# Eight joint VectorE sums per tile moved ahead of chosen multiplies in a pairwise-interaction recommender kernel

## The chip, the cores and the metric

The kernel runs on one core of one Trainium2 chip. The metric is the device time of one execution in microseconds (us). A core has five engines that run side by side and meet through semaphores: TensorE (PE, with its weight loads shown as PEld), VectorE (DVE), ScalarE (ACT), GpSimd (POOL) and SyncE (SP), which here only issues transfers.

## What is computed

32 table lookups per row give embeddings of 64 numbers, every pair of fields is combined through its own 64 x 64 matrix into one number, and the 496 numbers with 16 dense ones pass a small network:

```
e = stack([tbl_f[ids[:, f]] for f in range(32)], axis=1)      # 1024 x 32 x 64, float32
p = e[:, ROW_IDX]; q = e[:, COL_IDX]                           # the 496 pairs of fields
z = einsum('bne,hne,bnh->bn', p, kernel, q)                    # kernel 64 x 496 x 64
h = concatenate([z, dense_ctx], axis=1)                        # 1024 x 512
h = maximum(h @ W_top1 + b_top1, 0)                            # 512 x 512
h = maximum(h @ W_top2 + b_top2, 0)                            # 512 x 256
y = h @ W_top3                                                 # 256 x 1
```

## The kernel before

**Tiles and blocks.** The batch of 1024 rows is worked off in 8 tiles of 128 rows, numbered 0 to 7. Within a tile the 496 pairs are cut into 32 blocks, numbered 0 to 31. For each block TensorE writes a product `u` of embeddings and pair matrices (`block_u`, lines 609 to 631) into one of three PSUM slots (`USLOTS = 3`), and VectorE multiplies the slot with the other embedding (`multiply`, lines 512 to 538). The slots are used in a fixed rotation, which also takes in the transposes of embeddings (`turn_part`, line 593, emptied by VectorE's `copy_turned`, line 503): TensorE may fill a slot when VectorE has emptied the use three places earlier (`slot_free`, line 587, on the semaphore `slot_emptied`), and VectorE waits for `slot_filled`.

**Two kinds of block.** The string in line 76 says which: "SSTTTSSSTSTTTSST" "TSTTSTSSSTTSSTST". A T ("turned") block's product goes to `prod_t` (line 520), and TensorE adds it up later with small matmuls (`pick_sums`, line 633). An S ("straight") block's product goes to a ring of eight buffers in `prod_s` (line 537); of its 14 or 16 results ScalarE adds up all but four, one instruction pair each (`sum_block`, lines 424 to 434), and VectorE adds up the last four. VectorE does that for two S blocks at a time in one reduction (`sum_two`, lines 540 to 552). The eight pairs of S blocks are (0,1), (5,6), (7,9), (13,14), (17,20), (22,23), (24,27), (28,30).

**Order on VectorE.** It is written out in the loops of lines 564 to 576: the multiplies in order of block, embedding copies at `FIRST_TURN_AT` (tile 0, ahead of the multiplies of blocks 0, 2, 4, 7, 10, 16, 21), `own_turns` (behind the multiplies of blocks 0, 5, 12 in tile 1, of 4 and 12 in later tiles) and `early_turn` (the next tile's first part, behind block 27, in tile 0 behind block 28), and `sum_two` behind the multiply that follows the second block of a pair. `sum_two` first waits on `slot_emptied`, the semaphore that VectorE's own multiplies raise, for the second block's multiply:

```
if n > 0 and not TURNED[n - 1] and S_INDEX[n - 1] % 2 == 1:
    sum_two(t, S_INDEX[n - 1] - 1)
```

**Order on TensorE.** Between the blocks stand bursts of other work (lines 727 to 750): the previous tile's hidden layers behind blocks 7, 9, 10, 12, 17 and 19 (`PHASES_AT`, line 677), the previous tile's last `pick_sums` and the transposes of its sums behind block 4 (`late_spread`, which waits for all of that tile's `sum_two` through `summed_v` and for ScalarE's `acc_copied`), and this tile's `pick_sums` behind blocks 23, 27 and 31. Behind the last tile come the last `pick_sums`, the transposes and the last network (lines 751 to 764). GpSimd issues one gather per field and tile (line 383), each behind a step of TensorE.

Of the kernel before, what the change touches and what calls it, by code (L numbers as in the profile page):

```python
# [83 lines left out]
TURNED = [t for _, t in PLAN]  # L84
NB = len(BLOCKS)
NT = sum(TURNED)
NS = NB - NT
# [3 lines left out]
S_INDEX = [n - T_INDEX[n] for n in range(NB)]  # L91
STRAIGHT_AT = [n for n in range(NB) if not TURNED[n]]
# [7 lines left out]
def parts_of(t):  # L100

    return (FIRST_PARTS, SECOND_PARTS)[t] if t < 2 else PARTS
# [8 lines left out]


ON_DVE = 4
USLOTS = 3
SRING = 8
H0S = 3
# [32 lines left out]
def places(n):  # L149


    b = BLOCKS[n]
    found = []
    for half, side in enumerate((b.lower, b.upper)):
        with_k = {at + d: 2 * m + half for m, at, w in side for d in range(w)}
        other = {p[0] + d: p[2 + half] + d for p in b.products for d in range(p[1])}
        found += [(half * SLOTS + s, with_k[s], other[s]) for s in range(b.slots)]
    return found


def act_slots(n):
    return [s for s, _, _ in places(n)][:HALVES * BLOCKS[n].slots - ON_DVE]

# [2 lines left out]
ACT_COLUMN = [sum(len(act_slots(k)) for k in range(n) if not TURNED[k]) for n in range(NB)]  # L166
ON_ACT = sum(len(act_slots(n)) for n in range(NB) if not TURNED[n])
STRAIGHT = ON_ACT + NS * ON_DVE
S_CHUNKS = (STRAIGHT + DENSE) // P
T_CHUNKS = NT * HALVES * SLOTS // P  # L170
DIRECT_FROM = 3
# [8 lines left out]
LAST_SHARED = ACT_COLUMN[LAST_STRAIGHT] + LAST_ON_ACT  # L180
CHUNKS = S_CHUNKS + T_CHUNKS
QUAD = 32
PICK = T_CHUNKS * P
assert (STRAIGHT + DENSE) % P == 0 and (NT * HALVES * SLOTS) % P == 0 and CHUNKS == 4

# [66 lines left out]
def used(t, n):  # L252

    return SLOT_USE["u", t, n] + 1
# [24 lines left out]
def build(nc, ids, tables, k_pairs, dense, w1, b1, w2, b2, w3, ident, pick, out):  # L279
    with ExitStack() as ctx:  # L280
        def sb(name, shape, dt=F32):
            return ctx.enter_context(nc.sbuf_tensor(name, shape, dt))

        def sem(name):
# [6 lines left out]
        prod_t = [sb(f"prod_t{s}", [P, HALVES * BANK]) for s in range(TRING)]  # L291
        h0 = [sb(f"h0_{t}", [P, STRAIGHT + DENSE]) for t in range(H0S)]
        h0_t = sb("h0_t", [P, CHUNKS, P])
# [11 lines left out]

        u_ps = [ctx.enter_context(nc.psum_tensor(f"u_ps{s}", [P, HALVES * BANK], F32)) for s in range(USLOTS)]
        side_ps = ctx.enter_context(nc.psum_tensor("side_ps", [P, 4, P], F32))
# [36 lines left out]
        last = TILES - 1  # L344
        h1_ps = [u_ps[SLOT_USE["u", last, n] % USLOTS][:, half * BANK:half * BANK + P]
                 for n in (NB - 3, NB - 2) for half in range(2)]
        h2_ps = [u_ps[SLOT_USE["u", last, NB - 1] % USLOTS][:, half * BANK:half * BANK + P] for half in range(2)]

        spread_ps = acc_ps[:, 4 - S_CHUNKS:]
        acc = acc_ps[:].rearrange("p c b -> p (c b)")  # L350

        def buffer(t, n):
            at = (t * NS + S_INDEX[n]) % SRING
            return prod_s[:, at * HALVES * BANK:(at + 1) * HALVES * BANK]
# [34 lines left out]
        def _(sp):  # L389
# [14 lines left out]
            def load_dense(t):  # L404
                sp.dma_start(h0[t % H0S][:, STRAIGHT:], dense[bass.ts(t, P), :]).then_inc(dense_loaded[t % H0S], 16)

# [95 lines left out]
        def _(dve):  # L502
            def copy_turned(t, part):
                at = SLOT_USE["turn", t, part]
                dve.wait_ge(slot_filled, at + 1)
                first, last = parts_of(t)[part]

                turned_half = u_ps[at % USLOTS][:].rearrange("p (h m b) -> p m h b", h=HALVES, b=P // 2)
                nc.vector.tensor_copy(emb_t[t % 2][:, first:last, :].rearrange("p m (h b) -> p m h b", h=HALVES),  # L509
                                      turned_half[:, :last - first]).then_inc(slot_emptied, 1)  # L510

            def multiply(t, n):
                at = SLOT_USE["u", t, n]
                dve.wait_ge(slot_filled, at + 1)
                u = u_ps[at % USLOTS][:].rearrange("p (h x) -> p h x", h=HALVES)
                if TURNED[n]:
                    at = t * NT + T_INDEX[n]
                    (_, _, i0, _), = BLOCKS[n].products
                    low = emb_t[t % 2][:, i0 // 2:i0 // 2 + LOW, :].rearrange("p k b -> p (k b)")
                    done = nc.vector.tensor_tensor(  # L520
                        prod_t[at % TRING][:].rearrange("p (h x) -> p h x", h=HALVES), u,
                        low.unsqueeze(1).to_broadcast([P, HALVES, BANK]), ALU.mult)
                else:
                    at = t * NS + S_INDEX[n]
                    if at >= SRING:

                        dve.wait_ge(summed_a, at - SRING + 1)
                    product = buffer(t, n).rearrange("p (h x) -> p h x", h=HALVES)
                    by_field = emb[t % EMBS][:].rearrange("p (f e) -> p f e", e=EMBED)
                    for s, w, lower, upper in BLOCKS[n].products:  # L530
                        cols = slice(s * EMBED, (s + w) * EMBED)
                        if lower == upper:
                            low = emb[t % EMBS][:, lower * EMBED:(lower + w) * EMBED]
                            low = low.unsqueeze(1).to_broadcast([P, HALVES, w * EMBED])
                        else:
                            low = by_field[:, lower:upper + 1:upper - lower]
                        done = nc.vector.tensor_tensor(product[:, :, cols], u[:, :, cols], low, ALU.mult)  # L537
                done.then_inc(slot_emptied, 1)

            def sum_two(t, k):  # L540

                first, second = STRAIGHT_AT[k], STRAIGHT_AT[k + 1]
                dve.wait_ge(slot_emptied, used(t, second))
                if (t, second) == (last, LAST_STRAIGHT):
                    upper = buffer(t, second)[:, BANK:BANK + (ON_ACT - LAST_SHARED) * EMBED]
                    nc.vector.tensor_reduce(h0[t % H0S][:, LAST_SHARED:ON_ACT],
                                            upper.rearrange("p (n e) -> p n e", e=EMBED), AX_X, ALU.add)
                step = HALVES * BANK + (BLOCKS[second].slots - BLOCKS[first].slots) * EMBED
                start = (t * NS + k) % SRING * HALVES * BANK + (SLOTS + BLOCKS[first].slots - ON_DVE) * EMBED
                column = ON_ACT + k * ON_DVE  # L550
                nc.vector.tensor_reduce(h0[t % H0S][:, column:column + 2 * ON_DVE].rearrange("p (k n) -> p k n", k=2),  # L551
                                        two_runs(start, step), AX_X, ALU.add).then_inc(summed_v, 1)

            def two_runs(start, step):

                both = prod_s[:, start:start + 2 * step] if start + 2 * step <= SRING * HALVES * BANK else None
                if both is None:
                    both = prod_s[:, start + ON_DVE * EMBED - step:start + ON_DVE * EMBED + step]
                    return both.rearrange("p (k x) -> p k x", k=2)[:, :, step - ON_DVE * EMBED:].rearrange(
                        "p k (n e) -> p k n e", e=EMBED)  # L560
                return both.rearrange("p (k x) -> p k x", k=2)[:, :, :ON_DVE * EMBED].rearrange(
                    "p k (n e) -> p k n e", e=EMBED)

            for t in range(TILES):
                for n in range(NB):
                    if t == 0 and n in FIRST_TURN_AT:
                        copy_turned(0, FIRST_TURN_AT[n])
                    multiply(t, n)
                    if t > 0 and n in own_turns(t):
                        copy_turned(t, own_turns(t)[n])  # L570
                    if early_turn(t, n):
                        copy_turned(t + 1, 0)
                    if n > 0 and not TURNED[n - 1] and S_INDEX[n - 1] % 2 == 1:
                        sum_two(t, S_INDEX[n - 1] - 1)
                if not TURNED[NB - 1]:
                    sum_two(t, NS - 2)
            dve.wait_ge(weights_loaded, 80)
            for m in (1, 3):
                dve.wait_ge(last_h1_mm, m + 1)
# [6 lines left out]
        def _(pe):  # L586
            def slot_free(at):

                if at >= USLOTS:
                    pe.wait_ge(slot_emptied, at - USLOTS + 1)  # L590
# [73 lines left out]
            def spread_straight(t, to):  # L664
                pe.wait_ge(dense_loaded[t % H0S], 16 * (t // H0S + 1))
                pe.wait_ge(summed_v, (t + 1) * NS // 2)
                pe.wait_ge(acc_copied, t + 1)
                for c in range(S_CHUNKS):
                    done = nc.tensor.transpose(to[:, c], h0[t % H0S][:, c * P:(c + 1) * P], id_sb[:])  # L669
# [141 lines left out]
```

## Time and profile before

| what | value |
|---|---|
| time, median of 3 runs (lowest, highest) | 391.89 us (391.51, 392.28) |
| the profiled execution | span 467.8 us, 13484 instructions; no other time is given for it |
| share of the span busy: PE, PEld, DVE, ACT, POOL | 86%, 64%, 76%, 72%, 52% |
| tile 0, from VectorE's first multiply to tile 1's | 19.1 to 95.0 us |
| tiles 1 to 6, from first multiply to first multiply | 52.5 to 52.9 us each |
| tile 7, first multiply to the end of its last sum | 410.9 to 458.5 us |

The span is the stretch from the first to the last instruction of one execution that was recorded; the median belongs to executions that were not. The recorded one is 75.9 us longer, so durations of single instructions are taken from it, and sums over it have to be carried over with care. "Busy" is the time in which an engine had at least one instruction running.

### The profile page before, as it was taken

Reading aid. Unit: us, or ns where it says so; the run is one execution under the profiler, and the core shown is the slowest. Engines: PE = TensorE matmul, PEld = TensorE weight load, DVE = VectorE, ACT = ScalarE, POOL = GpSimd, SP = SyncE. Lnnn points to the kernel's source line nnn. Section 1 sums busy time; section 2 is a strip of 40 time slices with the busy share of each in tenths; the row PEclk is TensorE's granted clock in tenths of the full one; section 3 lists DMA queues with packets and bytes.
Section 4 is the critical chain, followed back from the end, with each engine's and each line's share of the span. In section 5 each row is a group of like instructions: output and inputs, shape, how many; then the busy total and the mean of one; then the engine's idle time right before and its main releaser. Section 6 shows DMA issues by size and latency. Waiting matters only on the chain.

```text
span 467.8 us, 13484 instructions
## 1 busy us (share of the span) xinstructions
PE 402.3 (86%) x4800; PEld 298.7 (64%) x4800; DVE 354.2 (76%) x449; ACT 335.2 (72%) x2889; POOL 241.7 (52%) x260
## 2 busy tenths in 40 slices
PE   0537869598898989999999989999999989999997
PEld 0425645467766776677756776677757776668765
DVE  0226757577888978887888978887887978888982
ACT  1216656658689685969689685969689685969894
POOL 5555555545555556555555555555555555552000
PEclk9978789799999999999999999999999999999999
DMA  3564560101111011101111011101111111110000
GB/s 73 180 207 158 165 190 18 21 18 22 22 24 22 19 24 22 23 22 22 21 26 21 20 24 22 23 20 22 22 23 24 20 24 22 22 21 15 2 2 1
DMA packets 14563, 19.27 MB, mean 41 GB/s; under 512 B 7192, under 2 KB 7840, under 8 KB 14496
## 3 DMA queue, kind: packets, MB, share of 16 engines
q0 software_dynamic: 8192, 8.40, 9.1%
q1 hardware_dynamic: 6304, 10.00, 6.7%
q8 instruction: 38, 0.62, 0.6%
q14 instruction: 29, 0.24, 0.2%
HBM read 18.39 MB, written 0.00 MB: 39 GB/s over the span
## 4 chain that ended last, share of the span: by engine, by line
PE 61%; DVE 18%; issue 9%; another core or an unknown queue 6%; ACT 3%; POOL 1%; DMA 1%; DVEq 0%
PE u_ps L628 24%; PE u_ps L621 20%; DVE prod_s L537 9%; PE side_ps L642 9%; DVE prod_t L520 6%; ACT prod_s L432 3%; PE side_ps L677 2%; PE u_ps L604 2%; PE acc_ps L677 2%; DVE h L551 2%; POOL emb L383 1%; PE u_ps L708 1%; PE side_ps L701 1%; DVE emb_t L509 1%
## 5 line engine op out<-in xcount | busy, mean ns | idle before, releaser
L432 ACT ACTIVATE prod_s<-prod_s 128x64 f32<-128x64 f32 x1405 | 307.9, 304 | 76.2 <-DVE prod_s L537 66.2
L383 POOL DMA_INDIRECT emb<-tbl,ids_sb x256 | 241.5, 943 | 184.5 <-issue 44.6
L432 ACT ACTIVATION_READ_ACCUMULATOR prod_s<-prod_s 128x1 f32 x1405 | 266.5, 230 | 3.6 <-issue 3.4
L520 DVE TENSOR_TENSOR prod_t<-u_ps,emb_t 128x1024 f32<-128x1024 f32 x128 | 154.1, 1219 | 54.7 <-remote 35.4
L621 PE MATMUL u_ps<-emb_t,k_sb 64*128 64x128 f32 x2048 | 159.1, 286 | 27.6 <-issue 13.9
L621 PEld LDWEIGHTS u_ps<-emb_t,k_sb 64*128 64x128 f32 x2048 | 146.2, 194 | 52.0 <-issue 29.6
L537 DVE TENSOR_TENSOR prod_s<-u_ps,emb 128x1024 f32<-128x1024 f32 (+4 forms) x224 | 150.8, 721 | 25.7 <-PE u_ps L628 11.7
L628 PE MATMUL u_ps<-k_sb,emb_t 64*128 64x512 f32 (+5 forms) x704 | 147.5, 503 | 15.1 <-DVE prod_s L537 10.5
L628 PEld LDWEIGHTS u_ps<-k_sb,emb_t 64*128 64x128 f32 x704 | 63.8, 196 | 51.8 <-issue 18.1
L642 PE MATMUL side_ps<-prod_t,pick_sb 128*32 128x256 f32 x1024 | 66.6, 387 | 0.1
L642 PEld LDWEIGHTS side_ps<-prod_t,pick_sb 128*32 128x32 f32 x1024 | 35.4, 111 | 21.4 <-issue 6.0
L677 PE MATMUL acc_ps<-h_t,w_sb 64*128 64x128 f32 x336 | 45.5, 276 | 0.2
L677 PE MATMUL side_ps<-h_t,w_sb 64*128 64x128 f32 x336 | 44.9, 274 | 0.0
L677 PEld LDWEIGHTS acc_ps<-h_t,w_sb 64*128 64x128 f32 x336 | 41.9, 188 | 4.3 <-remote 3.9
L551 DVE TENSOR_REDUCE h<-prod_s 128x8 f32<-128x512 f32 x64 | 43.3, 676 | 0.0
L677 PEld LDWEIGHTS side_ps<-h_t,w_sb 64*128 64x128 f32 x336 | 42.1, 188 | 0.2
L509 DVE COPY emb_t<-u_ps 128x512 f32<-128x512 f32 (+2 forms) x29 | 21.5, 740 | 24.8 <-PE u_ps L604 21.6
L604 PE MATMUL u_ps<-id_sb,emb 64*128 64x64 f32 x256 | 16.0, 235 | 19.6 <-DMA emb<-tbl,ids_sb 17.3
L604 PEld LDWEIGHTS u_ps<-id_sb,emb 64*128 64x128 f32 x256 | 12.6, 144 | 26.7 <-issue 22.1
L459 ACT ACTIVATE h_t<-side_ps,b_sb 128x128 f32<-128x128 f32 x7 | 2.6, 367 | 17.0 <-PE side_ps L677 17.0
L469 ACT ACTIVATE y_row<-side_ps 1x128 f32<-1x128 f32 x8 | 2.1, 266 | 14.2 <-issue 9.0
L448 ACT ACTIVATE h_t<-side_ps 128x512 f32<-128x512 f32 x7 | 4.2, 598 | 9.6 <-PE side_ps L669 9.6
(27 smaller groups left out, 43.5 us busy)
## 6 DMA issues: line engine op xcount, KB each, us to landing
k_sb<-k_pairs SPq DMA_DIRECT2D x9, 512.0 KB, 4.5
emb<-tbl,ids_sb POOLq DMA_INDIRECT x256
k_sb<-k_pairs SPq DMA_DIRECT2D x6, 480.0 KB, 5.0
w_sb<-w SPq DMA_DIRECT2D x1, 1024.0 KB
w_sb<-w SPq DMA_DIRECT2D x1, 512.0 KB
k_sb<-k_pairs SPq DMA_DIRECT2D x1, 448.0 KB
h<-dense SPq DMA_DIRECT2D x8, 8.0 KB
out<-y_row SPq DMA_DIRECT2D x8, 0.5 KB
```

Source lines behind the costliest of these rows:

```text
L383: nc.gpsimd.indirect_dma_start(emb[t % EMBS][:, f * EMBED:(f + 1) * EMBED], None, tables[f], bass.IndirectOffsetOnAxis(ap=ids_sb[:, t, f:f ...
L432: done = nc.scalar.activation(slot, slot, ACT.Copy, accum_out=to[:, column:column + 1])
L509: nc.vector.tensor_copy(emb_t[t % 2][:, first:last, :].rearrange("p m (h b) -> p m h b", h=HALVES), turned_half[:, :last - first]).then_in ...
L520: done = nc.vector.tensor_tensor(prod_t[at % TRING][:].rearrange("p (h x) -> p h x", h=HALVES), u, low.unsqueeze(1).to_broadcast([P, HALVE ...
L537: done = nc.vector.tensor_tensor(product[:, :, cols], u[:, :, cols], low, ALU.mult)
L551: nc.vector.tensor_reduce(h0[t % H0S][:, column:column + 2 * ON_DVE].rearrange("p (k n) -> p k n", k=2), two_runs(start, step), AX_X, ALU. ...
L604: done = nc.tensor.transpose(u[:, at:at + P // 2], emb[t % EMBS][rows, 2 * m * EMBED:(2 * m + 2) * EMBED], id_sb[rows, rows])
L621: done = nc.tensor.matmul(u[:, half * BANK + d * P:half * BANK + (d + 1) * P], k_sb[rows, K_AT[n] + d * P:K_AT[n] + (d + 1) * P], emb_t[t ...
L628: done = nc.tensor.matmul(u[:, half * BANK + s * EMBED:half * BANK + (s + w) * EMBED], emb_t[t % 2][rows, m], k_sb[rows, K_AT[n] + s * EMB ...
L642: done = nc.tensor.matmul(side_ps[quad:quad + QUAD, :T_CHUNKS].rearrange("p c b -> p (c b)"), pick_sb[:, 30 - 2 * place:62 - 2 * place], p ...
L677: done = nc.tensor.matmul(to[m], weights[rows, c, m * P:(m + 1) * P], x[rows, c], start=(not swapped and c == 0), stop=(swapped and c == 3))
L701: done = nc.tensor.matmul(side_ps[0:1, LOGIT], w3_sb[:, c:c + 1], h2_t[:, c], start=(c == 0), stop=(c == 1))
```

## The change

The reductions are no longer tied to the multiply behind a pair. A table gives for each of eight blocks the pair that is summed ahead of its multiply:

```diff
 ON_DVE = 4
+
+
+SUMS_BEFORE = {2: 0, 8: 2, 10: 4, 15: 6, 21: 8, 24: 10, 28: 12, 31: 14}
 USLOTS = 3
...
+assert sorted(SUMS_BEFORE.values()) == list(range(0, NS, 2))
+assert all(STRAIGHT_AT[k + 1] < n for n, k in SUMS_BEFORE.items())
...
                 for n in range(NB):
                     if t == 0 and n in FIRST_TURN_AT:
                         copy_turned(0, FIRST_TURN_AT[n])
+                    if n in SUMS_BEFORE:
+                        sum_two(t, SUMS_BEFORE[n])
                     multiply(t, n)
                     if t > 0 and n in own_turns(t):
                         copy_turned(t, own_turns(t)[n])
                     if early_turn(t, n):
                         copy_turned(t + 1, 0)
-                    if n > 0 and not TURNED[n - 1] and S_INDEX[n - 1] % 2 == 1:
-                        sum_two(t, S_INDEX[n - 1] - 1)
-                if not TURNED[NB - 1]:
-                    sum_two(t, NS - 2)
```

The key is the block whose multiply follows, the value the pair's first S index: 0 is the pair (0,1), 2 is (5,6), and so on to 14 for (28,30). No instruction is added or removed.

## Rows read from the trace of the kernel before

**Rows 1.** The page, parts 1 and 2: busy time and slices.
```profile
span 467.8 us, 13484 instructions
PE 402.3 (86%) x4800; PEld 298.7 (64%) x4800; DVE 354.2 (76%) x449; ACT 335.2 (72%) x2889; POOL 241.7 (52%) x260
```

**Rows 2.** Windows: head, tiles 0, 1, 3 and 7, tail; columns in the first line.
```profile
core 0: us, PE busy (x) PEld busy (x) DVE busy (x) ACT busy (x) POOL busy (x), PEclk, DMA share, GB/s
0.00:19.10 19.10, 4.08 (x22) 2.85 (x22) 0.69 (x1) 1.28 (x1) 11.66 (x16) 1.00 0.43 122
19.10:92.50 73.40, 49.60 (x443) 35.22 (x446) 44.45 (x59) 40.50 (x351) 39.62 (x42) 0.82 0.42 129
...
200.10:252.90 52.80, 49.07 (x609) 37.05 (x607) 43.96 (x57) 41.69 (x365) 30.18 (x33) 1.00 0.11 22
...
410.90:457.70 46.80, 45.70 (x605) 33.77 (x601) 41.92 (x55) 40.45 (x359) 9.05 (x10) 1.00 0.04 9
457.70:467.80 10.10, 7.09 (x62) 6.05 (x62) 1.83 (x5) 3.14 (x16) 0.00 (x0) 1.00 0.01 2
```

**Rows 3.** Timeline of VectorE, tile 3: start, length, what, [idle before it].
```profile
204.23 1.23 DVE L520 TENSOR_TENSOR prod_t<-u_ps,emb_t 128x1024 f32<-128x1024 f32 x1 [1.90 <-remote]
205.38 0.68 DVE L551 TENSOR_REDUCE h<-prod_s 128x8 f32<-128x512 f32 x1
205.97 2.35 DVE L520 TENSOR_TENSOR prod_t<-u_ps,emb_t 128x1024 f32<-128x1024 f32 x2
...
218.00 1.22 DVE L520 TENSOR_TENSOR prod_t<-u_ps,emb_t 128x1024 f32<-128x1024 f32 x1 [2.32 <-remote]
...
234.36 1.23 DVE L520 TENSOR_TENSOR prod_t<-u_ps,emb_t 128x1024 f32<-128x1024 f32 x1 [1.08 <-PE u_ps L628]
235.50 0.68 DVE L551 TENSOR_REDUCE h<-prod_s 128x8 f32<-128x512 f32 x1
...
239.17 1.23 DVE L537 TENSOR_TENSOR prod_s<-u_ps,emb 128x1024 f32<-128x1024 f32 x1 [0.73 <-PE u_ps L628]
```

**Rows 4.** VectorE's waits (us in total, times, longest): first and last of 14 rows.
```profile
DVE prod_t L520 <- remote: 35.4, 15, 5.4
...
DVE prod_s L537 <- issue: 0.2, 1, 0.2
```

**Rows 5.** The chain that ended last, tile 2, two stretches: start, length, what.
```profile
161.81 1.22 DVE prod_s L537
163.03 2.30 another core or an unknown queue
...
165.35 1.22 DVE prod_t L520
166.58 0.59 DVE h L551
167.17 1.16 DVE prod_t L520
168.32 0.04 issue
...
199.47 0.26 DVE h L551
```

**Rows 6.** Timeline of ScalarE, an instruction that waits for ScalarE's own semaphore.
```profile
205.43 0.25 ACT L432 ACTIVATION_READ_ACCUMULATOR prod_s<-prod_s 128x1 f32 x1
205.71 0.19 ACT L439 ACTIVATE h<-acc_ps 128x20 f32<-128x20 f32 x1
```

**Rows 7.** Timelines of VectorE, TensorE and ScalarE at the end.
```profile
456.41 1.22 DVE L520 TENSOR_TENSOR prod_t<-u_ps,emb_t 128x1024 f32<-128x1024 f32 x1
456.80 1.53 PE L642 MATMUL side_ps<-prod_t,pick_sb 128*32 128x256 f32 x20
458.74 0.38 ACT L491 ACTIVATE h_t<-side_ps 128x256 f32<-128x256 f32 x1
```

## The prediction

> **What bounds the kernel now.** I read the page first [rows 1]. TensorE is busy for 402.3 us, which is more than the 391.9 us that an unrecorded run takes in all, so the recorded execution is not the one that is timed: TensorE must be quicker outside it. VectorE's 354.2 us in only 449 instructions are 76% of the span, but 90% of 391.9. Both readings matter, because the change only reorders VectorE.
>
> Next the windows [rows 2]. In tile 3, which stands for tiles 1 to 6, VectorE is busy for 43.96 of 52.80 us and sits idle for 8.8. In tile 7 it is idle for 4.9, in tile 0 for 29.0 (73.40 less 44.45). Before its first multiply it is idle for 18.4 us and after its last for 8.3.
>
> Then VectorE's timeline [rows 3]. It shows where the idle time stands in a tile: 1.90 us ahead of the multiply of block 2 and 2.32 ahead of block 10, 1.08 ahead of block 21 and 0.73 ahead of block 24, the same blocks in every tile from 1 to 6. These are four of the seven places whose order really changes. Everywhere else the engine runs without a gap, and the next instruction starts before the record of the last one ends: 234.36 + 1.23 is 235.59, the sum starts at 235.50, 0.09 earlier.
>
> Last the chain [rows 5]. Per tile it crosses VectorE behind the stall at block 10: multiply, sum (0.59), multiply of block 11, and then TensorE, which waited for that slot. A second sum is on it at the end of the tile, ahead of the next tile's block 0. The other six lie beside it.
>
> **Which of the two readings holds outside the record.** Suppose VectorE's instructions last as long there. Then 391.9 - 354.2 leaves 37.7 us of idle time. Head and tail take 18.4 + 8.3 = 26.7, which leaves 11.0; each of the 88 waits in the view of waits [rows 4] also breaks one 0.09 us overlap, so at most another 7.9 comes back. That is at most 19 us for eight tiles, where the record has 29.0 in tile 0 alone and 58 in the others (six of 8.8 and one of 4.9). Part of tile 0's is the first gathers, which stay. If tile 0 keeps 14, tiles 1 to 7 have about 5 us between them, 0.7 per tile. So outside the record VectorE is nearly saturated, and I take it as the bound. A saturated engine gains nothing from another order of the same work; it loses whatever the new order adds.
>
> **The change part by part.** Nothing is added or removed: 64 reductions of 0.59 us from start to start before and after [rows 3, 5]. The pair (5,6) was summed behind the multiply of block 7 and is now summed ahead of block 8's, which is the same place: no change. The other seven go ahead of one multiply.
>
> *The new wait.* `sum_two` waits for VectorE's own multiply of the pair's second block. Before, another multiply stood between, so the condition was long met. Now it follows directly: ahead of blocks 2, 10, 15, 21, 24 and 31 in every tile; ahead of block 28 in tiles 0 and 7 only (in the others the copy of the next tile's embeddings lies between); and in tile 0 not ahead of 2, 10 and 21, where an embedding copy lies between. That makes 4 in tile 0, 36 in tiles 1 to 6, 7 in tile 7. No row shows VectorE waiting for itself. The nearest is ScalarE doing so [rows 6]: the writer ends at 205.68, the waiter starts at 205.71, 0.03 later. On VectorE that means a start 0.03 after the record's end in place of 0.09 before it: 0.12 us each. From below the bound is 0 (a wait cannot bring a start forward), from above 0.14, with the 0.04 and 0.01 of rounding that TensorE needs after VectorE [rows 5]. I take 0.12, the same kind of wait. In tiles 1 to 7: 43 x 0.12 = +5.2 us. Tile 0's four fall where it waits for TensorE anyway, the waits of its own: 0, at most +0.5 without that cover. Queued behind each held sum is the next multiply, and behind that TensorE's slot.
>
> *A rule against that price.* The Trainium skill, "VectorE: DVE Perf Modes", section "The DRAIN you can't avoid", says that eight chained copies take the same time with a semaphore after each as with one after the last, so the semaphore is free. The rows above show a next start 0.09 ahead of the recorded end, which a wait for that end has to give up. By the page this term would be 0 and not +5.2.
>
> *Idle time that is filled.* A sum ahead of a multiply that would have waited costs nothing, and what follows comes 0.59 us earlier. Of tile 3's idle time, 1.90 + 2.32 + 1.08 + 0.73 = 6.0 of 8.8 us stand at the changed places, about two thirds. Of the 5 us that I leave for tiles 1 to 7 that is 3.3. Some comes back as a later wait, since TensorE is nearly as loaded; I take -2.5, with bounds 0 and -6.6 (if 10 us of idle are left). In tile 0 the sums ahead of blocks 10 and 28 meet waits: between 0 and 2 x 0.59, taken as -0.6.
>
> *Multiplies that come later.* Seven multiplies per tile start 0.59 + 0.12 later. TensorE refills a slot three uses on, two multiplies of 1.13 (1.22 less 0.09) later; with three slots this is covered while VectorE is the slower side: 0. ScalarE gets blocks 24 and 28 later; its ring of eight buffers covers it. `summed_v` is raised earlier, but `late_spread` looks at it only after the next tile's block 4: 0. GpSimd's gathers follow TensorE's steps and SP is not passed: 0.
>
> *The end.* In tile 7 the multiply of block 31 [rows 7] starts 0.71 later, and with it the last small matmuls, which end at 458.33, and ScalarE's copy of them, which starts at 458.74. The 0.41 between them is mostly ScalarE's own order, so 0.3 to 0.7 is exposed: +0.5.
>
> *Sum.* 5.2 - 2.5 - 0.6 + 0.5 = +2.6 us, so 391.9 + 2.6 = 394.5. The sum is made against the median, because the record's span of 467.8 has the idle time that the timed runs can't have; against the span the same steps give the first rival.
>
> **The rivals.**
>
> *A: the recorded idle time is real, only scaled.* Then the sum at block 10 leaves the chain (-0.59 per tile) and the one at the tile's end stays and gets its wait (+0.12): -0.47 x 7 = -3.3 us, 388.6. For it: the waits sit at exactly these blocks in every tile. Against it: the balance of idle time above. It decides from the point where tiles 1 to 7 keep more than 5.2 us of idle at the changed places outside the record, 0.75 per tile. Chance 0.20.
>
> *B: VectorE is saturated and the wait on itself is free.* Then only the filled idle time is left: -2.5 - 0.6 + 0.5 = -2.6, so 389.3, or 391.9 if there is none to fill. The page above would have it so. Against it: ScalarE's row. Chance 0.15.
>
> *C: slots come back too late.* A later multiply before a burst of TensorE (blocks 24 and 31) starves VectorE after it. Price: 0.59 per tile on top of 2.6, 7 x 0.59 = 4.1, so 398.6. For it: TensorE is busy for 49.07 of 52.80 us. Against it: sums that follow the burst's blocks made room before as well. Chance 0.07.
>
> *The change does not do what it says.* Only for the pair (5,6), one of eight.
>
> **How the numbers follow.** My forecast, saturated with a priced wait, has 0.58; within it the terms run from +5.7 + 0.7 (398.3) down to full idle recovery, 5.2 - 6.6 - 1.2 + 0.3 = -2.3 (389.6), most of it between 392.8 and 397. About 0.2% (0.8 us) is what a measurement can tell here. Faster: nearly all of A, most of B, a little of the forecast: 0.31. Same: 0.04 of B and about 0.12 of the forecast: 0.16. Slower: the rest, 0.53. The range leaves out the far half of A and of C: 388.5 to 398.0.
>
> **What would show it.** In the recorded profile of the changed kernel: sums at L551 with an idle time of about 0.03 before them (right if 0.02 to 0.06, rule of the page right if they still overlap); the wait ahead of block 10 down from 2.32 to about 1.6, and tiles 1 to 6 shorter by some 0.5 us, so that the span falls to about 464.5 even where the time rises. If span and time both fall by more than 3 us, A is right and my balance of idle time was wrong. If the time does not move and the sums show their 0.03, the filled idle time is larger than I took it. A span that grows by 4 us or more speaks for C.

## The result and the profile after

| | before | after |
|---|---|---|
| median, four runs each | 391.7 us (389.83 to 392.28) | 394.61 us (393.55 to 396.26) |
| ratio | | 1.0083, 95% interval 1.006 to 1.0106 |
| recorded execution, span | 467.8 us [rows 1] | 391.7 us (its time 393.55) |

The change costs 2.9 us, 0.8%. The forecast was 394.5 with slower as the likeliest sign. The number came out; a good part of the working behind it did not, as the experiments show.

The first thing to see is the span. The record of the changed kernel is as long as its timed run, and 76 us shorter than the record of the kernel before. A reorder that makes the kernel slower cannot have done that, so rows 1 to 7 can't be laid beside the new record line by line. The first experiment below repeats the kernel before and gives a record that can.

The page of the changed kernel, parts 1 and 2 (busy us, share and count; then tenths in 40 slices):

```profile
span 391.7 us, 13484 instructions
PE 361.0 (92%) x4800; PEld 279.8 (71%) x4800; DVE 353.0 (90%) x449; ACT 330.8 (84%) x2889; POOL 242.1 (62%) x260
PE   0457899999999999999999999999999999999987
DVE  0248999899999999999999999999999999999981
```

VectorE's busy time is what it was in [rows 1] (354.2), TensorE's is 41.3 us less, and both stand at eight or nine tenths from the sixth slice to the last but one. The waits of VectorE (us in total, times, longest) are five rows and 23 waits instead of 14 rows and 88 [rows 4]; the "remote" group of 35.4 us is gone:

```profile
DVE emb_t L514 <- PE u_ps L607: 18.6, 10, 15.0
DVE prod_s L542 <- PE u_ps L631: 6.0, 7, 2.0
DVE prod_t L525 <- PE u_ps L624: 3.3, 3, 2.2
```

The timeline of VectorE in tile 3 (start, length, what, idle before it), to be read against [rows 3]:

```profile
172.00 1.21 DVE L542 TENSOR_TENSOR prod_s<-u_ps,emb 128x1024 f32<-128x1024 f32 x1
173.24 0.69 DVE L556 TENSOR_REDUCE h<-prod_s 128x8 f32<-128x512 f32 x1
173.84 3.48 DVE L525 TENSOR_TENSOR prod_t<-u_ps,emb_t 128x1024 f32<-128x1024 f32 x3
...
191.76 0.69 DVE L556 TENSOR_REDUCE h<-prod_s 128x8 f32<-128x512 f32 x1
192.36 1.21 DVE L542 TENSOR_TENSOR prod_s<-u_ps,emb 128x1024 f32<-128x1024 f32 x1
...
197.22 1.22 DVE L514 COPY emb_t<-u_ps 128x1024 f32<-128x1024 f32 x1 [0.25 <-PE u_ps L607]
198.36 0.67 DVE L556 TENSOR_REDUCE h<-prod_s 128x8 f32<-128x512 f32 x1
198.95 1.21 DVE L542 TENSOR_TENSOR prod_s<-u_ps,emb 128x1024 f32<-128x1024 f32 x1
200.08 1.21 DVE L525 TENSOR_TENSOR prod_t<-u_ps,emb_t 128x1024 f32<-128x1024 f32 x1
```

Block 9's multiply ends at 172.00 + 1.21 = 173.21 and the sum behind it starts at 173.24: 0.03 after the end, as forecast from ScalarE's row. The waits of 1.90, 2.32, 1.08 and 0.73 us are all gone; the only listed one in the tile is 0.25 us ahead of the copy behind block 27. The tile lasts 44.29 us (first multiply at 159.96, next tile's at 204.25), as do tiles 2 to 6.

### The profile page after: what moved, and what is told of

Read it like the earlier page. It is cut to its first block, busy times and chain, and to the rows that moved or that the text cites. A ratio compares the mean times of both kernels' runs of the same rounds, so it can differ in the third digit from the quotient of the medians.

```text
span 391.7 us, 13484 instructions
## 1 busy us (share of the span) xinstructions
PE 361.0 (92%) x4800; PEld 279.8 (71%) x4800; DVE 353.0 (90%) x449; ACT 330.8 (84%) x2889; POOL 242.1 (62%) x260
## 4 chain that ended last, share of the span: by engine, by line
PE 80%; DVE 9%; issue 4%; POOL 4%; DMA 3%; ACT 0%
PE u_ps L624 26%; PE u_ps L631 24%; PE side_ps L645 15%; PE side_ps L680 5%; PE acc_ps L680 5%; DVE prod_s L542 4%; POOL emb L388 4%; DMA emb<-tbl,ids_sb 3%; PE u_ps L607 2%; DVE prod_t L525 2%; DVE h L556 2%; PE u_ps L711 1%; PE side_ps L704 1%; DVE emb_t L514 1%; PE side_ps L672 1%
## 5 line engine op out<-in xcount | busy, mean ns | idle before, releaser
L437 ACT ACTIVATION_READ_ACCUMULATOR prod_s<-prod_s 128x1 f32 x1405 | 270.1, 257 | 0.0
L525 DVE TENSOR_TENSOR prod_t<-u_ps,emb_t 128x1024 f32<-128x1024 f32 x128 | 151.0, 1214 | 3.3 <-PE u_ps L624 3.3
L624 PEld LDWEIGHTS u_ps<-emb_t,k_sb 64*128 64x128 f32 x2048 | 131.3, 190 | 23.8 <-issue 8.3
L624 PE MATMUL u_ps<-emb_t,k_sb 64*128 64x128 f32 x2048 | 136.7, 277 | 5.8 <-DVE prod_s L542 2.9
L631 PE MATMUL u_ps<-k_sb,emb_t 64*128 64x512 f32 (+5 forms) x704 | 131.6, 484 | 1.8 <-DVE emb_t L514 0.8
L645 PE MATMUL side_ps<-prod_t,pick_sb 128*32 128x256 f32 x1024 | 63.3, 382 | 1.0 <-DVE prod_t L525 1.0
L645 PEld LDWEIGHTS side_ps<-prod_t,pick_sb 128*32 128x32 f32 x1024 | 32.0, 109 | 22.3 <-issue 3.2
L607 PE MATMUL u_ps<-id_sb,emb 64*128 64x64 f32 x256 | 14.8, 234 | 19.5 <-DMA emb<-tbl,ids_sb 19.4
L704 PEld LDWEIGHTS side_ps<-h_t,w_sb 128*1 128x1 f32 x32 | 2.0, 82 | 6.4 <-issue 5.3
L704 PE MATMUL side_ps<-h_t,w_sb 128*1 128x128 f32 x32 | 4.8, 271 | 0.5 <-DVE h_t L586 0.5
```

The costliest lines, as they stand in the source:

```text
L437: done = nc.scalar.activation(slot, slot, ACT.Copy, accum_out=to[:, column:column + 1])
L525: done = nc.vector.tensor_tensor(prod_t[at % TRING][:].rearrange("p (h x) -> p h x", h=HALVES), u, low.unsqueeze(1).to_broadcast([P, HALVE ...
L607: done = nc.tensor.transpose(u[:, at:at + P // 2], emb[t % EMBS][rows, 2 * m * EMBED:(2 * m + 2) * EMBED], id_sb[rows, rows])
L624: done = nc.tensor.matmul(u[:, half * BANK + d * P:half * BANK + (d + 1) * P], k_sb[rows, K_AT[n] + d * P:K_AT[n] + (d + 1) * P], emb_t[t ...
L631: done = nc.tensor.matmul(u[:, half * BANK + s * EMBED:half * BANK + (s + w) * EMBED], emb_t[t % 2][rows, m], k_sb[rows, K_AT[n] + s * EMB ...
L645: done = nc.tensor.matmul(side_ps[quad:quad + QUAD, :T_CHUNKS].rearrange("p c b -> p (c b)"), pick_sb[:, 30 - 2 * place:62 - 2 * place], p ...
```

## The experiments

Single timed runs of one kernel spread over 0.4 to 0.8%, but where a record is clean (its span fits its timed run and shows no long stalls) its tiles 2 to 6 are equal to 0.01 us, so the length of such a tile is the finer measure. It is read as the distance of the first multiplies of two tiles.

### The kernel before, once more (e1_before_again)

No edit.

> The kernel before, run once more for a record to lay beside that of the changed kernel, whose span is 391.7 us. Theory (VectorE saturated, each wait on itself costs 0.12 us): time within 0.2% of before; where the record is not stretched, tiles 2 to 6 last 44.25 - 6 x 0.12 = 43.5 us each against 44.25 after the change, VectorE's idle time in them under 1 us, every sum starts 0.08 to 0.09 before the end of the multiply ahead of it. Rival (the waits ahead of blocks 2, 10, 21 and 24 are real): idle time of 1 us and more stands ahead of these blocks here too and the tile is as long as after the change or longer.

391.31 us, ratio 0.9998 (0.9981 to 1.0016), span 389.4 us. Tiles 2 to 6 last 43.96 us, 0.33 less than after the change, where the expectation had 43.5 and 0.75 less. The windows of tile 3 in this record and in that of the changed kernel (columns as in [rows 2]):

```profile
159.76:203.71 43.95, 43.95 (x609) 34.61 (x608) 43.27 (x56) 41.20 (x368) 30.25 (x33) 1.00 0.13 26
```
```profile
159.96:204.25 44.29, 43.92 (x609) 34.54 (x607) 43.79 (x55) 41.22 (x368) 30.19 (x32) 1.00 0.13 26
```

Before, TensorE's records leave no gap, and VectorE is idle for 0.68 us: 0.56 ahead of block 24 and 0.12 ahead of block 5, nothing ahead of 2, 10 and 21. The prediction's balance of idle time had put 0.7 us there. But the engine with no visible gap is TensorE, and the chain of tile 3 says the same. The shares by line, from its head, hold not one VectorE line:

```profile
by line: PE u_ps L621 33.8%; PE u_ps L628 33.3%; PE side_ps L642 16.8%; PE side_ps L677 6.6%; PE acc_ps L677 5.7%; PE u_ps L604 2.9%; PE side_ps L701 0.9%; PE side_ps L669 0.8%
```

Both views have to be read with care. Most of TensorE's matmul records here last 0.27 us while the next pair starts after 0.11, so they overlap, and a pause of a few tenths of a us leaves no gap and puts nothing on the chain. The weight loads, whose records are shorter, show such a pause in the kernel before, ahead of block 31:

```profile
198.07 1.21 DVE L537 TENSOR_TENSOR prod_s<-u_ps,emb 128x1024 f32<-128x1024 f32 x1
199.34 0.97 PEld L621 LDWEIGHTS u_ps<-emb_t,k_sb 64*128 64x128 f32 x16 [0.46 <-DVE prod_s L537]
```

Block 28's multiply ends at 199.28 and block 31's product starts 0.06 us behind it. Blocks 3 and 4 start just as closely behind the multiplies of blocks 0 and 1 (161.01 behind 160.96, 162.07 behind 162.02). So before the change, too, TensorE waits for VectorE's slots, briefly and at the same places in every tile.

After the change the chain leaves TensorE once per tile (start, length, what):

```profile
196.53 0.66 PE u_ps L607 x16
197.19 0.02 issue
197.22 0.04 DVE emb_t L514
197.25 1.10 issue
198.36 0.67 DVE h L556
199.03 1.14 DVE prod_s L542
200.18 0.04 issue
200.22 1.16 PE u_ps L624 x16
```

and TensorE's timeline shows the gap it leaves there, its weight load the whole wait:

```profile
198.82 1.03 PE L631 MATMUL u_ps<-k_sb,emb_t 64*128 64x64 f32 x6
200.22 1.16 PE L624 MATMUL u_ps<-emb_t,k_sb 64*128 64x128 f32 x16 [0.37 <-DVE prod_s L542]
```
```profile
200.22 0.19 PEld L624 LDWEIGHTS u_ps<-emb_t,k_sb 64*128 64x128 f32 x2 [0.99 <-DVE prod_s L542]
```

This is the costly place. TensorE transposes the next tile's embeddings (to 197.19), does blocks 28, 29 and 30, and for block 31 needs the slot that block 28's multiply empties. VectorE has the copy, now the sum of (24,27), then that multiply. The sum used to stand behind the multiply; now its 0.59 us lies in the path, and TensorE's records show a gap of 0.37 us. From the first matmul of block 30 to that of block 31 it is 1.40 us here and 0.87 in the kernel before: 0.53 lost.

The tile is only 0.33 longer, because part of this comes back and a little more is lost elsewhere. The same distance of first matmuls, read through all of tile 3, is 0.16 us shorter after the change for each of the blocks 3 and 4 (1.05 to 0.89 and 1.06 to 0.90), 0.10 longer for block 18 (1.76 to 1.86) and 0.03 longer for block 19 (1.10 to 1.13). Block 18 needs the slot of block 15, whose multiply now stands behind a sum with its wait. All other distances of the tile agree to 0.01 us. 0.53 - 0.32 + 0.13 is 0.34.

### The places without the waits (e2_lagged)

```diff
+SUMS_BEFORE = {2: 0, 8: 2, 10: 4, 15: 6, 21: 8, 24: 10, 28: 12, 31: 14}
...
+                    if n in SUMS_BEFORE and (t, n) != (0, 2):
+                        lagged = SUMS_BEFORE[n] - 2
+                        sum_two(t if lagged >= 0 else t - 1, lagged if lagged >= 0 else NS - 2)
                     multiply(t, n)
...
+            sum_two(last, NS - 2)
```

> The sums stand where the change puts them, but each takes the pair before, whose multiplies are long done (the pair (28,30) of a tile is summed ahead of the next tile's block 2, the last one behind everything). So the place is that of the change and the wait is gone. Theory (the wait is the cost): the time of before, 391.7 us, plus at most 0.6 us at the end; tiles 2 to 6 last 43.5 us and no sum has idle time ahead of it. Rival C (the place costs, since slots come back later): still 393.9 to 395 us, with idle time of VectorE ahead of multiplies and none ahead of sums.

393.03 us, ratio 1.0032 (1.0012 to 1.0053); tiles 2 to 6 last 44.15 to 44.16 us. No sum has idle time ahead of it, and still the tile is 0.20 us longer than before. The chain has the same detour:

```profile
196.89 0.66 PE u_ps L605 x16
197.55 0.02 issue
197.57 0.04 DVE emb_t L510
197.61 1.10 issue
198.71 0.68 DVE h L552
199.39 1.14 DVE prod_s L538
```

So the place costs by itself, which the prediction had at nothing and which its rival C held. By the distances of first matmuls the 0.20 are the whole 0.53 lost at block 31, less the 0.32 that comes back at blocks 3 and 4. With the waits the tile is 44.29, so the six waits, 0.11 us each, 0.66 together, add 0.13, and they add it at blocks 18 and 19.

### The waits without the places (e3_old_place_wait)

```diff
-            def sum_two(t, k):
+            def sum_two(t, k, behind):
...
-                dve.wait_ge(slot_emptied, used(t, second))
+                dve.wait_ge(slot_emptied, used(t, behind))
...
+                        sum_two(t, S_INDEX[n - 1] - 1, n)
```

> The sums stand where they stood before the change, but each waits for the multiply just ahead of it, which it does not read: eight waits of VectorE on itself per tile and no change of place. Theory: 8 x 0.12 = 0.96 us per tile over the kernel before, 43.5 + 0.96 = 44.5 us, in all tiles 1 to 7 +6.7 us, 398.4 us. Rival C (the place costs): no change, 391.7 us. The rule by which a semaphore costs nothing: no change as well.

`behind` is the block that was multiplied last. 395.3 us, ratio 1.0101 (1.007 to 1.0131); 44.59 us per tile, 0.63 over before where 0.96 was expected. The sum that follows block 10's multiply, in the same timeline view:

```profile
173.55 1.22 DVE L520 TENSOR_TENSOR prod_t<-u_ps,emb_t 128x1024 f32<-128x1024 f32 x1
174.79 0.69 DVE L551 TENSOR_REDUCE h<-prod_s 128x8 f32<-128x512 f32 x1
```

174.77 to 174.79 is again a start just behind the end. With eight such waits most of the chain of this tile is VectorE's (33.1% and 29.1% its products), and the distance to TensorE's first matmul of block 3 is 0.26 us longer than before. The missing 0.3 us went into the idle time VectorE had: its 0.12 at block 5 is gone, and 0.43 of the 0.56 at block 24 is left. So a wait of VectorE on itself costs the engine 0.11 us, and the kernel pays it once VectorE's slack is used up. The Trainium skill, "VectorE: DVE Perf Modes", "The DRAIN you can't avoid", has eight chained copies in which a semaphore after each costs nothing extra. This run has a cost where each sum waits for the multiply just ahead, and here the measurement decides.

### Three of the seven places (e4_three_moved)

```diff
+SUMS_BEFORE = {10: 4, 21: 8, 24: 10}
```

> Only the sums of three pairs are moved, to ahead of blocks 10, 21 and 24, the places where the first record showed the longest waits; three waits on itself per tile in place of six. Theory: 3 x 0.12 = 0.36 us per tile, tiles 2 to 6 last 43.85 us, +2.5 us less what tile 0 gives back, 393 to 394 us. Rival A (filled idle time is worth 0.47 us per tile): 389 us or less.

390.48 us, ratio 0.9986 (0.9965 to 1.0007): no difference that can be told. 43.90 us per tile, 0.06 under before. The waits are there (sums 0.03 behind their multiplies), the 0.56 ahead of block 24 is gone, 0.25 has appeared ahead of the copy. TensorE's records have no gap. Both the price (0.36) and rival A's gain (0.47) missed: the three waits and the filled idle time change when TensorE gets a slot only at block 31, 0.05 us sooner than before.

### Four kernels on a slower chip (e5 to e8)

Of the change only block 24 (e5); the pair (17,20) at block 24 (e6); three idle times filled, with the pair (22,23) behind block 27 (e7, three lines); the other four places (e8):

```diff
+SUMS_BEFORE = {24: 10}
...
+SUMS_BEFORE = {24: 8}
...
+SUMS_BEFORE = {5: 0, 24: 8}
...
+                    if n == 27:
+                        sum_two(t, 10)
...
+SUMS_BEFORE = {2: 0, 15: 6, 28: 12, 31: 14}
```

> Of the change only the sum of the pair (22,23) ahead of block 24, where the clean record of the kernel before shows the only sizeable idle time in a tile, 0.56 us. Theory (a wait on itself costs 0.11 where VectorE runs without a gap; a place pays back only the idle time that stands at it): tiles 2 to 6 last 43.96 - 0.65 + 0.11 + about 0.34 (the 0.25 us wait that moved to the copy of the next tile's embeddings with three sums moved, and its overlap), 43.7 to 43.8 us, so two waits fewer than the 43.90 us of three sums moved; 389.5 to 390.5 us. Rival (the places at blocks 10 and 21 gave the gain there, not block 24): 43.96 us or more.

> The idle time ahead of block 24 is filled by the sum of the pair (17,20), which comes from behind block 21 and whose multiplies are long done; all else as before. No wait on itself. Theory: 0.11 us per tile less than with the pair (22,23) there, 43.6 to 43.7 us per tile, the sum starts with idle -0.08; 389 to 390 us. If the wait on itself did not matter beside the place, both kernels have the same tile.

> Three sums in three idle times, none of them just behind its own multiply: (0,1) ahead of block 5 (0.12 us of idle), (17,20) ahead of block 24 (0.56), (22,23) behind block 27 and ahead of the copy (0.25). If VectorE is the bound, the tile falls towards 43.1 us, its length without idle time: 43.2 to 43.5 us, so 387 to 389 us, faster than both kernels. If TensorE takes over before that, idle time turns up ahead of other multiplies and the tile stays at 43.6 us or more.

> The rest of the change: the sums ahead of blocks 2, 15, 28 and 31, with the other moved ones (10, 21, 24) left where they were. Three waits on itself per tile in tiles 1 to 6. If the parts add up, the tile is 44.29 - 43.90 + 43.96 = 44.35 us, slower than with the whole change, +2.7 us in tiles 1 to 7. The theory prices 0.34 us of the 0.39 with the three waits; rival C (late slots) would show new idle time ahead of block 0, 1 or the copy at block 27.

These four ran on a chip where the kernel before takes 462.28 us, median of 35 runs. The ratios are 1.0014 (1.0004 to 1.0024), 0.9997 (0.9987 to 1.0006), 0.9992 (0.9983 to 1.0002) and 1.0014 (1.0001 to 1.0028): for these four orders the time moved by 0.14% at most. They answered nothing on the expected tile lengths, but their records look like the first record. The page of e6 and two timelines of its tile 3:

```profile
span 461.8 us, 13484 instructions
PE 396.0 (86%) x4800; PEld 291.7 (63%) x4800; DVE 353.4 (77%) x449; ACT 334.4 (72%) x2889; POOL 241.7 (52%) x260
```
```profile
202.02 1.23 DVE L521 TENSOR_TENSOR prod_t<-u_ps,emb_t 128x1024 f32<-128x1024 f32 x1 [1.74 <-remote]
```
```profile
201.86 0.94 PE L624 MATMUL u_ps<-emb_t,k_sb 64*128 64x128 f32 x11 [0.93 <-issue]
```

They repeat [rows 1] and the 1.90 us ahead of block 2 of [rows 3]. TensorE pauses for 0.93 us in the middle of block 3, after 5 of its 16 matmul records, and waits for nothing that the record shows. VectorE's multiply of block 2 starts only behind this pause, at 202.02, although the last matmul record of its product ends at 200.43; so by this record the two engines stop together, and VectorE's wait is not one for TensorE's work. The record of the kernel before looks like this; the runs that it was timed by do not. That it fell on such a chip is the likeliest reading; where it ran is not on record. What makes the engines pause is open. The granted clock doesn't account for it: 0.974 in the record of e6 and 0.971 in that of the kernel before, against 1.000 in e1, under 3% for a span that is 19 to 20% longer.

### Two of them again (e9_three_filled_again, e10_other_four_again)

> The same kernel as e7_three_filled, whose run fell on a chip where the kernel before takes 462.3 us in place of 391.6. Where before takes 391.6: tiles 2 to 6 at 43.2 to 43.5 us against 43.96, sums with idle -0.08, 387 to 389 us, if VectorE is the bound; 43.6 us or more, with new idle time ahead of other multiplies, if TensorE takes over first. Where before takes 462 us: no difference over 0.2%.

> The same kernel as e8_other_four (the sums ahead of blocks 2, 15, 28 and 31 moved, the others left), for the same reason. Where before takes 391.6 us: 44.35 us per tile in tiles 2 to 6 if the parts of the change add up, of the 0.39 us over before 0.34 by three waits of VectorE on itself; new idle time ahead of the copy at block 27 or ahead of blocks 0 and 1 speaks for the place as a cost of its own. Where before takes 462 us: no more than 0.2%.

Now before took 391.62 us. **e9** took 392.97, ratio 1.004 (1.0025 to 1.0054), 44.20 us per tile: a miss, slower instead of 2 to 4 us faster. Its timeline around block 24:

```profile
188.83 2.34 DVE L538 TENSOR_TENSOR prod_s<-u_ps,emb 128x1024 f32<-128x1024 f32 x2
191.09 0.67 DVE L552 TENSOR_REDUCE h<-prod_s 128x8 f32<-128x512 f32 x1
192.33 1.22 DVE L538 TENSOR_TENSOR prod_s<-u_ps,emb 128x1024 f32<-128x1024 f32 x1 [0.56 <-PE u_ps L633]
```

The idle time stands where it stood, at its 0.56 us, behind the sum. That sum had stood two multiplies earlier, so what VectorE does ahead of block 24 is the same work in another order. Idle time is filled only by work from behind it. And 0.49 us of idle time is new ahead of the copy behind block 4.

What makes this kernel slower is the sum of (0,1), brought from behind block 2 to ahead of block 5: it now stands behind the new idle time, so everything after it comes later. From first matmul to first matmul TensorE loses 0.18 us at and just behind block 14 and 0.08 at block 17, whose products start 0.06 us behind VectorE's multiplies; together 0.26, the tile's 0.24. Yet TensorE counts as busy for all of tile 3:

```profile
160.02:204.22 44.20, 44.20 (x609) 34.51 (x608) 43.15 (x56) 41.19 (x368) 30.16 (x33) 1.00 0.13 26
```

So a TensorE that is busy for the whole of a tile in this view is no proof that its own work sets the tile's length.

**e10** took 396.03 us, ratio 1.0124 (1.0097 to 1.0151). Its tile of 44.35 us is what the parts add up to. The sign that was named for rival C, new idle time ahead of the copy or of blocks 0 and 1, is hardly there (0.04 ahead of block 0); the lost time is TensorE's. Its chain passes through the same copy, sum and multiply as that of the whole change, with TensorE idle for 0.43 us ahead of block 31 in the view of idle times:

```profile
198.52 0.98 issue
199.51 0.67 DVE h L552
200.18 1.14 DVE prod_s L538
201.32 0.04 issue
201.36 1.16 PE u_ps L622 x16
```

Copy and sum follow each other with no wait on itself there, so the loss sits with these four places and not with the waits at 10, 21 and 24: 0.59 more than before at block 31 and 0.13 at blocks 18 and 19, less 0.32 at blocks 3 and 4.

### Block 24 alone, and with block 27 (e11_only_24_again, e12_24_and_27)

```diff
+SUMS_BEFORE = {24: 10}
...
+                    if n == 27:                      # e12_24_and_27 only
+                        sum_two(t, 12)
                     if early_turn(t, n):
```

> The same kernel as e5_only_24 (only the sum of (22,23), ahead of block 24). The run that filled idle time with sums from before it gained nothing, since the idle time just stayed behind them; this one brings a sum from behind the idle time to ahead of it. Where before takes 391.6 us: three sums moved gave 43.90 us per tile, the two at blocks 10 and 21 stand where VectorE has no idle time and cost 2 x 0.115, so 43.67 us, 0.29 under before, -2.0 us, 389.6 us. Rival (the places at 10 and 21 helped): 43.9 us or more. Where before takes 462 us: no more than 0.2%.

> The same and the sum of (24,27) brought from behind block 28 to behind block 27, ahead of the copy of the next tile's embeddings, where 0.25 us of idle time stood in the runs with block 24's sum moved. Theory: that idle time and its overlap (0.33) go, one more wait of VectorE on itself comes (0.115): 43.67 - 0.22 = 43.45 us per tile, 388 us. Rival (late slots): the copy and what TensorE does behind it come later and idle time stands ahead of blocks 28 to 1 in its place: 43.67 us or more. Where before takes 462 us: no more than 0.2%.

**e11**: 391.27 us against 391.89, ratio 0.9996 (0.998 to 1.0011), 43.90 us per tile, not 43.67, which is what its rival had. It equals e4 although it has two waits fewer, so the places at 10 and 21 neither help nor cost: without their waits VectorE only has 0.37 us of idle time ahead of the copy in place of 0.25. **e12**: 390.51 us, ratio 0.9967 (0.9951 to 0.9983), 43.82 us per tile, not 43.45; the rival's sign is there, 0.17 us of idle time ahead of block 0. It is faster than before by 0.3% and 4.1 us under the changed kernel, and it moves the very sum that costs in the change, but one place further up, to before the copy, so that copy and multiply of block 28 follow each other. The window of its tile 3 has TensorE's records without a gap and VectorE idle for 0.36 us:

```profile
160.27:204.09 43.82, 43.82 (x610) 34.49 (x607) 43.46 (x55) 41.06 (x367) 30.18 (x32) 1.00 0.14 26
```

That is not TensorE's own work either. The table gives, for tile 3 of the clean records, how much longer the distance of first matmuls is than the shortest of the nine, in us; the entries from 0.05 up stand where a block starts 0.05 to 0.10 us behind the multiply that frees its slot, or just behind such a block. The shortest distances are 0.89 and 0.90 us (blocks 3 and 4), 1.79, 0.76 and 1.03 (14, 15, 17), 1.75 and 1.10 (18, 19) and 0.82 (31).

| | blocks 3 and 4 | 14, 15 and 17 | 18 and 19 | 31 | together | tile | tile less these |
|---|---|---|---|---|---|---|---|
| before (e1) | 0.32 | 0.01 | 0.01 | 0.05 | 0.39 | 43.96 | 43.57 |
| the change | 0 | 0.02 | 0.14 | 0.58 | 0.74 | 44.29 | 43.55 |
| e2, places without waits | 0 | 0.02 | 0 | 0.58 | 0.60 | 44.15 | 43.55 |
| e3, waits without places | 0.59 | 0.14 | 0.14 | 0.17 | 1.04 | 44.59 | 43.55 |
| e4 and e11 | 0.33 | 0.02 | 0.01 | 0 | 0.35 | 43.90 | 43.55 |
| e9, three filled | 0.33 | 0.26 | 0 | 0.05 | 0.64 | 44.20 | 43.56 |
| e10, other four | 0 | 0.01 | 0.14 | 0.64 | 0.79 | 44.35 | 43.56 |
| e12, 24 and 27 | 0 | 0.02 | 0 | 0.24 | 0.26 | 43.82 | 43.56 |

The last column is the same to 0.02 us in all, so these few waits for slots are the whole difference between the kernels. It is also an upper bound for TensorE's own work, since blocks 17 and 19 start just behind VectorE's multiplies in all nine. VectorE is busy for 43.27 us of the tile in e1, so neither engine is the bound by itself. What comes back at blocks 3 and 4 does so in the kernels where VectorE is idle ahead of block 0 (0.04 us in the change and e10, 0.17 in e2 and e12), that is, where block 0 comes late enough for VectorE to have caught up.

## Why the prediction was right, and where it was not

- **The recorded execution is not the one that is timed.** Right, and confirmed by e1. "TensorE must be quicker outside it" was right too, but recording as such is not the cause: the kernel's record in e1 is as long as its timed run. The likeliest cause is the chip that the first record fell on.
- **The reading of the first record.** "Everywhere else the engine runs without a gap" does not hold: in tile 3 of that record 1.14 us stand ahead of the copy behind block 27, 0.72 ahead of block 14 and 0.50 ahead of block 8, and the 1.08 ahead of block 21 is 0.36 to 0.37 in tiles 1, 2 and 4 to 6. The window taken for tile 0 ends 2.5 us before tile 0 does.
- **The balance of idle time.** Right in size, partly by luck: 0.7 us per tile was forecast, and 0.68 is there in tiles 2 to 6. But VectorE's idle time is 1.7 us in tile 1 and 1.8 in tile 7, 8.1 in tile 0 where 14 was put, and its busy time is 348.9 us and not 354.2.
- **"VectorE is nearly saturated, and I take it as the bound."** This step failed. Nearly saturated it is (43.27 of 43.95 us), but TensorE is as nearly so: without its longer waits for slots the tile would last 43.57 us. What a reorder costs or gives is decided at the few blocks where TensorE waits for VectorE (3, 4, 18, 19 and 31). The prediction took TensorE's 402.3 us as proof that it was quicker elsewhere and did not ask how close it came there.
- **The new wait, 0.12 us each.** The price and the count were right on the engine: 0.11 us, six per tile. The exposure was wrong. 5.2 us were charged; by e2 against the change 0.13 us per tile are, 0.9 us in seven tiles.
- **Idle time that is filled, -2.5 us.** It was filled, the 0.56 us at block 24. It was worth 0.06 us per tile (e4, e11), -0.4 us in seven. What the change does win back is another wait, TensorE's ahead of blocks 3 and 4: 0.32 us per tile, 1.9 in tiles 2 to 7, near the 2.5 by chance.
- **Multiplies that come later, 0.** Wrong, and the largest part of what is lost: 0.53 us per tile at block 31, 3.2 us in tiles 1 to 6, or 0.20 per tile net of blocks 3 and 4, without any wait of VectorE on itself (e2). "With three slots this is covered while VectorE is the slower side" was the argument, and at block 31 it is not. I checked blocks 24 and 31, the ones ahead of bursts; the one that costs is 28, where copy, sum and multiply stand in a row.
- **The end, +0.5 us.** From block 30's multiply to the end of the program it is 12.46 us before (376.94 to 389.4) and 13.1 after (378.61 to 391.7): +0.6, right. The last small matmuls wait 1.03 us for block 31's multiply.
- **Tile 0, -0.6 us.** It can't be told: between its first multiply and tile 1's it lasts 52.19 us before and 51.90 after, but 51.07 to 53.18 over all clean records.
- **The marks.** The span was to fall to 464.5 with 1.6 us left ahead of block 10; that was read off the slow record and is void.

In the two clean records: tiles 2 to 6 give 5 x 0.33 = 1.7 us, tile 1 0.3 (46.09 against 45.77), tile 7 and the end 0.8 together, tile 0 and the head -0.5; 2.3 us of the spans' 389.4 and 391.7. By place: 3.2 at block 31 and 0.9 at blocks 18 and 19 lost, 1.9 at blocks 3 and 4 won back, 0.6 lost at the end and 0.5 won in tile 0 and the head. The median says 2.9. So 394.5 against 394.61 is in part luck: a term that was much too large (+5.2 for the waits, 0.9 measured) stood in for one that was missing (the late slot at block 31, 3.2), and the -2.5 met a gain of about its size at a place that the prediction had not named.

Rival A fell with the stalls, which are not in the timed runs. Rival B fell on the 0.03 us start. Rival C had the right mechanism at the wrong blocks: at block 31 alone its price of 0.59 is nearly met (0.53), for the tile as a whole it is too high (0.20 to 0.33).

What was not tried: the change with the sum of (24,27) alone put back. That this sum is the one that costs rests on the chains of the change, e2 and e10, all three through it (in e2 the sum at this place is that of another pair), on e4 and e11, which leave it and lose nothing at block 31, and on e12, which moves it ahead of the copy and loses 0.24 there.

## What to carry to other kernels

A gap on an engine is filled only by work that stood behind it, and filling it pays only where another engine then gets its buffer sooner; where two engines are within 2% of each other, check both before taking one as the bound. A busy share of 100% in matmul records hides waits of a few tenths of a us here; the distances from first matmul to first matmul, or the weight loads, show them. A piece of work that moves ahead of the instruction that frees a buffer costs where the other engine is waiting for that buffer, here mainly at one place of seven (0.53 us), and a little at a second (0.13). Before reading a record, compare its span with the timed runs: one that is 19% longer showed stalls here, in the same places in every tile, that the timed program does not have.

## What the runs showed of the hardware

- An instruction of VectorE that waits for the one just ahead starts 0.03 us after the recorded end in place of 0.08 to 0.09 before it. Eight such waits in a 44 us tile cost the kernel 0.63 us (e3); three cost it nothing (e4).
- A matmul of TensorE that waits for a slot starts 0.05 to 0.06 us after the recorded end of VectorE's multiply (blocks 3, 4, 17, 19 and 31 of e1).
- One program, the kernel before, took 391.6 to 391.9 us (medians) on three chips and 462.3 us on a fourth, with most executions of each within 1%. Between its own two records VectorE's busy time hardly differs (354.2 and 348.9 us), TensorE's does (402.3 against 362.0), at a granted clock of 0.971 and 1.000; of the 78 us 24 fall into tile 0. In e6 the pause inside a block is 0.93 us long.
- An order of the sums that costs 1.24% on one of the fast chips (e10) costs 0.14% there (e8, the same kernel).
